# Gate softmax sums and value copies moved to ScalarE, with new step orders in the last two attention passes

## What is computed

```
x = _layernorm(x + _L0_attn_ref(x, ...))              # pass A: 16 heads of 16
x = _layernorm(x + _L0_xattn_ref(x, ctx, ctx, ...))   # pass B: 77 keys
x = _layernorm(x + _L0_ffn_ref(x, ...))               # pass B: quantized 256 -> 1024 -> 256
x = _layernorm(x + _L1_attn_ref(x, ...))              # pass C: rotary attention
x = _layernorm(x + _L1_xattn_ref(ctx, x))             # alignment by dynamic programming
x = _layernorm(x + _L1_ffn_ref(x, ...))               # pass D: attention with a gate per token
```

```
gates = softmax(h @ Wr.T + br)           # 15 routed heads; the 3 largest are kept, times 3
sw = softmax(h @ Ws.T + bs)              # 2 values
weight_0 = sw * 2.0
shared = weight_0[..., 0:1] * sw
routed = weight_0[..., 1:2] * (gates * mask * 3)
out = h * concat([shared, routed]).sum(-1, keepdims=True)
return out @ Wp.T + bp
```

## Time and profile before

| | us |
|---|---|
| median of 3 runs | 6091.51 (6087.66 to 6099.28) |
| the profiled execution | 6097.69, its span 6095.9 |
| PE, DVE, ACT, POOL busy, share of the span | 88%, 84%, 67%, 42% |
| pass A, from the span's start to about | 1200 |
| pass B, to about | 2700 |
| pass C, to about | 4250 |
| alignment, to about | 4460 |
| pass D, to the end | 6096 |

### The profile page before, as it was taken

How to read it: one execution, slowest core, us unless ns; L and a number is a source line. 1 busy time by engine, 2 the same in 40 slices (tenths; PEclk the granted TensorE clock), 3 DMA queues, 4 the chain that set the end, 5 groups by cost and what they waited for, 6 DMA issues and landing times. The chain is left out here.

```text
span 6095.9 us, 142938 instructions
## 1 busy us (share of the span) xinstructions
PE 5354.1 (88%) x54914; PEld 3828.5 (63%) x54914; DVE 5140.5 (84%) x12191; ACT 4107.7 (67%) x7345; POOL 2546.5 (42%) x2574
## 2 busy tenths in 40 slices
PE   6999999879999999969999999998049999999998
PEld 4666666646666666647777777776036666666665
DVE  6888888769999999977777777776859999999997
ACT  5777777658888888866666666665336666666665
POOL 0111111223333333334444444444037677667765
PEclk9999999989999999989999999999569999999999
DMA  1111111110000000010010101010100000000000
GB/s 53 48 43 48 43 48 43 43 32 29 26 28 29 29 29 28 27 41 21 28 33 29 33 29 33 29 32 25 34 22 25 25 29 25 25 25 29 26 25 22
DMA packets 140392, 194.40 MB, mean 32 GB/s; under 512 B 25808, under 2 KB 63696, under 8 KB 139344
## 3 DMA queue, kind: packets, MB, share of 16 engines
q1 hardware_dynamic: 139728, 185.26, 9.7%
HBM read 113.03 MB, written 72.18 MB: 30 GB/s over the span
## 5 line engine op out<-in xcount | busy, mean ns | idle before, releaser
L1008 ACT ACTIVATE Dpr<-pj 128x512 f32<-128x512 f32 x1024 | 528.7, 602 | 255.0 <-PE pj L802 254.6
L1175 DVE TENSOR_REDUCE Amp<-pj 128x2 f32<-128x512 f32 x1024 | 630.9, 685 | 65.0 <-PE pj L869 65.0
L1175 DVE TENSOR_REDUCE Cmp<-pj 128x2 f32<-128x512 f32 x1024 | 638.7, 682 | 49.7 <-PE pj L869 49.7
L1008 ACT ACTIVATE Apr<-pj 128x512 f32<-128x512 f32 x1024 | 522.1, 613 | 205.8 <-PE pj L802 205.8
L1008 ACT ACTIVATE Cpr<-pj 128x512 f32<-128x512 f32 x1024 | 528.8, 602 | 184.6 <-PE pj L802 184.6
L1175 DVE TENSOR_REDUCE Dmp<-pj 128x2 f32<-128x512 f32 x1024 | 644.8, 682 | 9.4 <-PE pj L869 7.2
L1109 POOL TENSOR_SCALAR Ave<-Amv 128x2 f32<-128x2 f32 x64 | 14.7, 229 | 981.2 <-DVE Amv L1242 981.2
L1109 POOL TENSOR_SCALAR Bve<-Bmv 128x2 f32<-128x2 f32 x128 | 29.3, 229 | 870.7 <-DVE Bmv L1242 870.7
L1081 POOL TENSOR_TENSOR Dnrm<-Dnrm,power 128x32 f32<-128x32 f32 x64 | 348.9, 5452 | 98.8 <-DVE Dnrm L1153 98.8
L1116 POOL TENSOR_SCALAR Dx<-Dres,Dmv,Drstd 128x256 f32<-128x256 f32 x256 | 312.6, 1230 | 28.9 <-POOL Drstd L1110 28.9
L1116 POOL TENSOR_SCALAR Bx<-Bres,Bmv,Brstd 128x256 f32<-128x256 f32 x256 | 312.7, 1230 | 28.6 <-POOL Brstd L1110 28.6
(11 more groups left out here) (311 smaller groups left out, 15426.9 us busy)
## 6 DMA issues: line engine op xcount, KB each, us to landing
Ax0T<-in_xT SPq DMA_DIRECT2D x64, 256.0 KB, 2.9
Ax<-in_x SPq DMA_DIRECT2D x64, 256.0 KB, 3.1
x_A_scratch<-Ax SPq DMA_DIRECT2D x64, 256.0 KB, 2.0
Bx<-x_A_scratch SPq DMA_DIRECT2D x64, 256.0 KB, 2.9
x_B_scratch<-Bx SPq DMA_DIRECT2D x64, 256.0 KB, 2.0
Cx<-x_B_scratch SPq DMA_DIRECT2D x64, 256.0 KB, 2.8
x_C_scratch<-Cqr SPq DMA_DIRECT2D x64, 256.0 KB, 2.0
Dx<-x_C_scratch SPq DMA_DIRECT2D x64, 256.0 KB
```

Of the source, the lines that this page charges most:

```text
L1008: ck.tell(act.activation(dst, ck.bank(step + (bank,))[0:n, :], ACT.Exp, scale=HD ** -0.5), "probs_ready", step)
L1175: ins = dve.tensor_reduce(dst, src, AX.X, ALU.max, negate=True)
```

## The change

Four edits:
1. `gate` and `mix`. VectorE takes the two maxima negated and no longer subtracts them; ScalarE gives them as bias to four exponentials a stream (two token tiles, 15 routed and 2 shared values each) and takes the row sums with `accum_out`. In `mix` two sums are gone, two reciprocals are one, two products are one, and two pairs of products are one `scalar_tensor_tensor` each: 5 links and one closing signal in place of 7 links.
2. `v` in passes C and D is copied out by ScalarE without the bias. The bias, the same for all keys, is added behind the attention: `oT` is two activations of 128x256 with a bias column each in place of one copy of 128x512. The bias columns are loaded once a pass by small DMAs (two a pass); the row broadcast is gone.
3. `Clock.wait` leaves out a wait for a value that the engine has already waited for. This holds for all passes and engines.
4. New tables for passes C and D. Those of A and B stay.

```
 "C": {
-    "pe": (828, 502, 606, 934, ... 727), "act": (...), "dve": (...), "pool": (434, 5, 331, 27), "sp": (1132, 1135, 600, 913)
+    "pe": (201, 307, 527, 528, ... 319), "act": (...), "dve": (...), "pool": (127, 431, 434, 5), "sp": (1213, 1532, 1535, 1000)
 "D": {
-    "pe": (729, 730, 405, 622, ... 304), ..., "sp": (1000, 1436)
+    "pe": (1217, 1218, 1327, 1219, ... 1116), ..., "sp": (536, 0)
...
     def wait(self, name, step, nth=-1):
-        self.eng.wait_ge(sems[name], base[name] + counts.at[step, name, nth])
+        value = base[name] + counts.at[step, name, nth]
+        if value > self.reached.get(name, 0):
+            self.reached[name] = value
+            self.eng.wait_ge(sems[name], value)
...
+    elif kind == "v" and att in ("A3", "A4"):
+        ck.wait_bank_full(step)
+        src = ck.bank(step)[:].rearrange("p (t h d) -> p t h d", t=QT, h=H)
+        ck.tell(act.activation(vv[s][:, :, :, 0:HD], src, ACT.Copy), "v_ready", step)
+    elif kind == "oT" and att in ("A3", "A4"):
+        ck.wait_bank_full(step)
+        for c in range(FC):
+            ins = act.activation(atT[s][:, c, :], ck.bank(step)[:, c * S:(c + 1) * S], ACT.Identity,
+                                 bias=tiles.col[att + "_bv"][:, c:c + 1])
+        ck.tell(ins, "attnT_ready", step)
...
     elif kind == "mix":                                   # ScalarE
         ck.wait("logits_ready", ("gate", att, b))
-        ins = act.activation(ex[s][:], lg[s][:], ACT.Exp)
+        for t in range(QT):
+            for i, (low, high) in enumerate(((0, H - 1), (H - 1, H + 1))):
+                ins = act.activation(ex[s][:, t, low:high], lg[s][:, t, low:high], ACT.Exp,
+                                     bias=gs[s][:, i, t:t + 1], accum_out=gs[s][:, 2 + i, t:t + 1])
...
     elif kind == "oproj":                                 # VectorE
+            ck.wait("mixed", ("mix", att, b))
...
     elif kind == "gate":                                  # VectorE
-        dve.tensor_reduce(gs 0 <- lg[0:nr], max); link(dve.tensor_reduce(gs 1 <- lg[nr:], max))
-        dve.tensor_tensor(lg[0:nr] - gs 0); dve.tensor_tensor(lg[nr:] - gs 1)
+        dve.tensor_reduce(gs 0 <- lg[0:nr], max, negate); dve.tensor_reduce(gs 1 <- lg[nr:], max, negate)
```

More of the change, by code:

```diff
@@ L305, in signals @@
             "gu": ["gated", "hid_ready"], "hq": ["dve_step"] * 3 + ["scale_ready"], "dist": ["dist_ready"],
-            "gate": ["logits_taken", "dve_step", "logits_ready"], "mix": ["dve_step"] * 7,
+            "gate": ["logits_taken", "logits_ready"], "mix": ["dve_step"] * 5 + ["mixed"],
         },
@@ L534, in __init__ @@
                 self.split = {n: sb(n + "_split", [P, D], BF16, where) for n in SPLIT_BIASES if n.startswith(att)}
+                self.col = {n: sb(n + "_col", [P, FC], F32, where) for n in VALUE_BIASES if n.startswith(att)}
                 keys, nt = KEYS[att], tiles_of(att)
@@ L1154, in do @@
                                   "norms2", step)
-                    elif kind == "v":
+                    elif kind == "v" and att in ("A1", "A2"):
                         ck.wait_bank_full(step)
@@ L1298, in do @@
                         nr = H - 1
-                        dve.tensor_reduce(gs[s][:, 0, :].unsqueeze(2), lg[s][:, :, 0:nr], AX.X, ALU.max)
-                        link(ck, dve.tensor_reduce(gs[s][:, 1, :].unsqueeze(2), lg[s][:, :, nr:H + 1], AX.X, ALU.max))
-                        dve.tensor_tensor(lg[s][:, :, 0:nr], lg[s][:, :, 0:nr],
-                                          gs[s][:, 0, :].unsqueeze(2).to_broadcast([P, QT, nr]), ALU.subtract)
-                        ck.tell(dve.tensor_tensor(lg[s][:, :, nr:H + 1], lg[s][:, :, nr:H + 1],
-                                                    gs[s][:, 1, :].unsqueeze(2).to_broadcast([P, QT, 2]), ALU.subtract),
-                                  "logits_ready", step)
+                        dve.tensor_reduce(gs[s][:, 0, :].unsqueeze(2), lg[s][:, :, 0:nr], AX.X, ALU.max, negate=True)
+                        ck.tell(dve.tensor_reduce(gs[s][:, 1, :].unsqueeze(2), lg[s][:, :, nr:H + 1], AX.X, ALU.max,
+                                                  negate=True), "logits_ready", step)
                     elif kind == "mix":
@@ L1316, in do @@
-                        link(ck, dve.reciprocal(gs[s][:, 6, :], gs[s][:, 3, :]))
-                        e0, e1 = (ex[s][:, :, nr + i:nr + i + 1].rearrange("p t o -> p (t o)") for i in range(2))
-                        dve.tensor_tensor(gs[s][:, 7, :], e0, gs[s][:, 6, :], ALU.mult)
-                        dve.tensor_tensor(gs[s][:, 8, :], e1, gs[s][:, 6, :], ALU.mult)
+                            ins = dve.max(top[s][:, t, :], ex[s][:, t, 0:nr])
+                        link(ck, ins)
+                        dve.reciprocal(gs[s][:, 5:7, :], gs[s][:, 2:4, :])
@@ L1329, in _ @@
+                        link(ck, dve.scalar_tensor_tensor(out=gs[s][:, 12, :], in0=gs[s][:, 7, :], scalar=2.0,
+                                                          in1=gs[s][:, 10, :], op0=ALU.mult, op1=ALU.mult))
+                        ck.tell(dve.tensor_tensor(gs[s][:, 15, :], gs[s][:, 11, :], gs[s][:, 12, :], ALU.add), "mixed", step)
                 walk(dve, "dve", do)
@@ L1353, in _ @@
                                   for n, t in tiles.row.items()]
+                        loads += [(t[:, c:c + 1].unsqueeze(1), io[n][None, c * P:(c + 1) * P].rearrange("o (p n) -> p o n", n=1))
+                                  for n, t in tiles.col.items() for c in range(FC)]
                         for dst, src in loads:
```

50 lines of the change are left out of this document (23 added, 27 removed).

## The result

The changed kernel takes 6027.22 us (median, 6024.27 to 6031.25), the kernel before in the same session 6092.19 (6087.66 to 6099.28): a ratio of 0.9893, 95% interval 0.9876 to 0.991, or 65 us less. I had forecast 31 less. The profiled executions differ by 72 us of span (6095.9 to 6023.9). Two launches of the experiments ran at a much lower granted clock (7104.06 us at 0.729, 8283.5 us at 0.607) and no ratio uses them.

The account below looks back on a forecast made before the run. DVE and the load ring were taken to bound pass D, PE close behind, and PE pass C. D -50, C +26, left-out waits -4 and D's end -3 sum to -31 us: 6060.5, forecast 6040 to 6078, wide range 6008 to 6117.

Parts of the forecast that it names:

- the ring: Pass D: ln on DVE, POOL's normalization, store, loads, then path on DVE; DVE waits 0.89 us a round for the load.
- The gate and the mix: DVE in D: gate 1.76 to 0.51 us, mix 3.01 to 1.4, saving 2.85 a round; one POOL hold adds 1.1.
- D's groups: PE's core-and-max sequences in D: one fewer saves 0.41 us a round; v's bank costs 0.25, core3's banks 0.1.
- "slower" rival: Pass D: mix ahead of shift0 delays DVE's oproj; two holds and late max3 cost +57, 6117 us; chance 0.18.
- The left-out waits: All passes: dropping repeated semaphore waits saves 4 us (0 to 25), as PE never sits idle for issue.
- Core, max, max, X: PE in C and D: a core step, two max steps and wait for the first exponential cost 1.96 us.
- the first rival: Both orders are good: D's round 23.27 us, -63; C loses nothing; -12 in A and B; 6016 us; chance 0.22.
- PE steps stretched by late partners: PE in D: oT, expand and max0 get shorter, together 0.55 us a round.
- the 0.3 passed on: Pass D: DVE's load wait goes, and with it PE's waits at expand and L757, together 0.3 us a round.
- The forecast +26: Pass C's new order: third group +0.42, q behind xT +0.1, max2 max3 core3 -0.09; net +0.43 us, 60 rounds.
- `max2 max3 core3`: PE in C: these reordered steps are free to take 1.36 us instead of 1.54; half taken, -0.09 a round.
- the signs that I had named: Right: D's round 23.4 to 23.6 us, DVE about 85% or less, no load wait, C's round 23.5 or more.

Follow-up runs that it names:

- orders alone: The kernel before with only the new tables of passes C and D, values' copies and gate as before: 6097.27 us, ratio 1.0003.
- the run with the third group: The changed kernel with PE's max2 and max3 of pass D put back behind core2, ahead of pv0: 6080.33 us, ratio 0.9973.

## Why the prediction was right or wrong

To find the failed step I measured, over 20 rounds in the middle of each pass, the time from the first `core` or `max` step of a group to the step that follows it (medians), and put everything else of the round in one column. "All else" and "round" are means of the same rounds; in D's old order three of the 20 hold a fall of the clock, so its row doesn't add up.

| D, us a round | `pv` behind core0 (before: core2) | other two groups | core alone | groups | all else | round |
|---|---|---|---|---|---|---|
| before | 1.97 | 1.97, 1.87 | 1.08 | 6.89 | 17.44 | 24.32 |
| orders alone | 2.32 | 1.96, 1.91 | 1.31 | 7.50 | 16.19 | 23.72 |
| D's old order, all else changed | 1.81 | 1.81, 1.81 | 1.08 | 6.51 | 17.65 | 24.39 (23.90 median) |
| changed | 2.09 | 1.81, 1.81 | 1.13 | 6.84 | 16.28 | 23.13 |

- **What bounds D** was right. DVE and the ring held it: with DVE relieved but the ring kept, a round at full clock is still 23.9, with the ring loosened and DVE full it is 23.7, and with both it is 23.1. Now PE holds it at 97.5%. What I did not see is that a wait of PE for the load can cost more than its length, through the granted clock: 22 us in one run, some 54 in another.
- **The gate and the mix** were sized about right: gate 0.51 forecast, 5218.91 to 5219.38 = 0.47 measured; mix 1.4 and one hold of 1.1 forecast, 2.34 with one hold measured; DVE's work 21 forecast, 20.4 measured. (The mix of before has sixteen instructions in seven groups, not seventeen in eight, which makes the spacing 0.123 and ten of them 1.23, still under the 1.4 that I took; six instructions of the new mix have two SBUF inputs, not five.) The Trainium skill's "GPSIMD Engine Reference", section Key points, would let an instruction with two SBUF inputs be held by POOL; here one of them is, in 60 of 64 rounds, for 1.15 us. Of the two held before, only the subtraction had two SBUF inputs; the other is a TENSOR_SCALAR with one (L1324), and no row shows in which mode it ran, so "the trace agrees" was shown for one of the two. `path`'s second instruction (L1214, two SBUF inputs) takes 0.48 us within POOL's 5.45 us power, 63 times in the kernel before, and in the run with the third group, where it meets a product of POOL, 1.23. So a hold goes with POOL's tensor products and sums in these rows, and moves with the timing.
- **ScalarE**: the four exponentials with their sums take 5221.83 - 5220.69 = 1.14 us instead of 0.254, +0.9 where I took +0.7; each sum has a 0.19 us instruction of its own. They cost next to nothing because no PE step asks for `core2`'s first bank so soon. Where one does, in the run with the third group, `core2` to `pv0` takes 2.37 instead of 1.81.
- **D's groups**: forecast -0.41 + 0.25 + 0.1 = -0.06 a round, measured 6.84 - 6.89 = -0.05. The sum was right, its parts not all. `max2 max3 core2 pv0` is 0.16 less than 1.97 (forecast 0.16). The hold by the bank of `v`, which I had at 0.25, shows in the weight loads (`[0.32 <-ACT Dv L1025]` at 5220.85). The bank of `oproj`, which I had as covered (done at 5.1, needed at 5.3), costs 2.09 - 1.81 = 0.28. That is a small form of my "slower" rival. The left-out waits paid for half of it: `core1` to `norm0` is 1.81, where it is 1.96 with the new order alone. "Core, max, max, X costs 1.96 however little the max steps take" was true only as long as ScalarE and PE worked through repeated waits, and what I held against the first rival, that this group "doesn't depend on sequencer work", was wrong.
- **The failed step in D** is "PE steps stretched by late partners ... together 0.55" with the 0.3 passed on. I had listed `oT`, `expand`, `max0` and L757: 0.85. Everything outside the groups fell by 17.44 - 16.28 = 1.16. Of it `expand` gave 0.4 (1.20 + 0.06 idle to 0.87), the `max` steps outside groups 0.24, L757's idle 0.21, both shifts 0.19, the gate's 0.19 and the transposes of `oT` and `qT` on PE 0.15; the norms (+0.22) took the excess back. The shifts and the gate I had not looked at. And `q` doesn't wait for `xT` (forecast +0.1). Together -1.19 a round in these 20 rounds and -1.27 over the whole pass, instead of -0.8; 63 rounds, -80 instead of -50. The head of D (-7) and its end (-3) make 90.
- **Seen by edits**, the same failure is a term that the sum put at nothing. The orders alone give -52 in D, the same as my forecast for all of it. Everything outside the groups falls by 1.25 there too, but DVE, still with its full work, puts 0.6 into the groups. I had DVE's relief only as what makes it "stop being the bound"; on top of the orders it gave 38 us more, and -14 and -23 by its two pieces in the old order.
- **C was right by accident.** Groups of a round, again as medians, by the `core` step in them; all else is 16.4 us in each of the four:

| C, us a round | core0, core1, core2, core3 | sum |
|---|---|---|
| before | 1.96, 1.96, 1.54, 1.54 | 7.00 |
| orders alone | 2.02, 1.96, 1.96, 1.83 | 7.77 |
| C's old order, all else changed | 1.81, 1.81, 1.45, 1.63 | 6.70 |
| changed | 1.81, 1.90, 1.81, 1.84 | 7.36 |

  The forecast +26 was for the order, which alone costs twice that, +51 (0.77 a round). The third group costs 0.42, just as forecast, and `q` waits for nothing (forecast +0.1). The step that failed is `max2 max3 core3`: it was to take 0.09 less and takes 0.29 more. The left-out waits, which I had at -4 in all, then hide the difference: C comes out at +25, or, the other way round, 17 less by the waits and 42 more by the order (1573.4 - 1531.6). As for the 0.29: the last bank of `core3` is now that of `pv0`, and ScalarE copies it only while `core3` runs. The weight loads stop behind the sixth, until that copy is done:

```profile
3525.25 1.68 PE L807 MATMUL pj<-Cq,Ck 32*128 32x256 f32 x16
3526.86 1.99 PE L775 MATMUL pj<-A_wk,CxT 128*128 128x256 f32 x8
```

```profile
3525.15 0.60 ACT L1018 ACTIVATE Cqk<-pj 128x512 f32<-128x512 f32 x1 [0.58 <-PE pj L827]
```

```profile
3525.80 0.72 PEld L807 LDWEIGHTS pj<-Cq,Ck 32*128 32x128 f32 x10 [0.25 <-ACT Cqk L1018]
```

From 2800 to 4200 this wait stands there 59 times (14.8 us), with the orders alone 58 times (19.8 us, `ACT Cqk L1013`), and never in the kernel before. So the cause is shown by the traces; no run undoes it alone.

- **The left-out waits** are the term wrongly sized by the largest factor: -4 forecast, -16 in C's old order and -23 in its new one. "PE never sits idle for issue" was the wrong row to read. The waits cost on the way from PE to ScalarE and back, where they show as part of a wait for exponentials. In D, in either order, they show nothing beyond what kernels with the same pass D differ by.
- The rival "both orders are good" had D nearer than the forecast and still too small: its round of 23.27 and -63 us are to be set against 23.01, counted as it was, and -80. The 23.27 of the table above is counted by exponentials and agrees by chance. C it had wrong. The rival "slower" named a real wait with too high a price: one hold and `oproj` late by 0.28, not 0.9.
- Of the signs that I had named, C's round (23.51) and DVE's missing wait for the load came true. D's round came out under 23.4, DVE is 88.8% busy, PE waits for `oproj`'s bank, which I had put among the signs of being wrong, and hardly for exponentials in D.
- The values' copy stays 0.60 on ScalarE against 0.68 on DVE. The Trainium skill's "ScalarE: Activation LUTs", rules for kernel authors, prefers VectorE for additions and products; no run here shows a loss from the move, and in D alone it gave 23 us. The halves of `oT` with a bias column take 0.84 instead of 0.60 (forecast +0.2).

## What to carry to other kernels

When engines hand banks round in turn, price an order by group times (first start to next start), not by idle or busy shares: late banks stretch a step and count as work, and the weight loads' waits name the bank. Where a ring and an engine both hold a round, loosen the ring first, or savings on the engine partly turn into waiting. Before calling parts non-additive, look at single rounds and at the clock beside them: a mean of 24.3 us was here fifty rounds of 23.9 and five of 28.2. Tables for two passes should be timed apart: here one was worth -80 and the other +42, and taking only the good one gives 5987 instead of 6027 us.

## What the runs showed of the hardware that I had not expected

- Waiting again for a semaphore value that was already reached isn't free: 0.06 us more from PE to ScalarE and 0.10 more back, 1.97 against 1.81 a group, 16 to 23 us in pass C.
- In pass D's old order with all other edits, nine waits of PE of 1.0 to 1.9 us for a late load were followed in five cases by 6.8 or 10.2 us at half the granted clock, which cost 22 us together. In the kernel before and the changed kernel, which have no such waits there, the clock stayed full in the middle of the pass.
- A sum with `accum_out` adds an instruction of 0.19 us behind each activation; pairs of 15 and of 2 values follow each other at 0.29 us alike.
- Eight bf16 `max` matmuls directly ahead of a `core` step delay it by only 0.22 us (5220.10 to 5220.32), though their own row lasts 0.40.
